# One more transfer per step and taller row-score matmuls in a one-core attention and FFN layer

## What is computed

```
xn = layernorm(x)
c_q, c_kv = xn @ Wq_down, xn @ Wkv_down          # latent 64
q_c, k_c, v_c = per head (128 heads) 4 features from the latents
q_r = xn @ Wq_rope  (128 heads x 64)             k_r = xn @ Wk_rope  (64, shared by all heads)
scores = (q_c . k_c + q_r . k_r) / sqrt(68)
out = softmax(scores) @ v_c, then @ Wo            -> s
g = silu(ffn(xn))                                 # low-rank adapted, tiled weights
y = x + s * g
```

## Time and profile before

| | us |
|---|---|
| median of 3 runs | 1936.92 |
| lowest, highest | 1936.13, 1938.21 |
| the profiled execution | 1934.79 |
| its span in the trace | 1932.6 |
| TensorE matmul busy | 1905.8 (99%) |
| VectorE busy | 1396.3 (72%) |
| ScalarE busy | 1028.6 (53%) |
| GpSimd busy | 467.9 (24%) |

### The profile page before, as it was taken

One profiled execution on the slowest core, in us unless ns is written; L12 is line 12 of the kernel. 1 busy time (PEld: TensorE's weight loads), 2 busy tenths in 40 slices (PEclk: granted clock), 3 DMA queues, 4 the chain that ended last, 5 costly groups with the idle time before them and its releaser, 6 DMA issues.

```text
span 1932.6 us, 37697 instructions
## 1 busy us (share of the span) xinstructions
PE 1905.8 (99%) x12464; PEld 1503.9 (78%) x12464; DVE 1396.3 (72%) x1644; ACT 1028.6 (53%) x1536; POOL 467.9 (24%) x790
## 2 busy tenths in 40 slices
PE   7999999999999999999999999999999999999999
PEld 5788777778777778777778877777877777777776
DVE  8787777777776777777777777777777777678665
ACT  5655555555555555555555555555555555555232
POOL 5422121222212131212122221213121212211231
PEclk9999999999999999999999999999999999999999
DMA  7622121221212121211121121212121212234331
GB/s 244 215 50 48 29 44 34 41 41 31 45 26 51 29 52 28 46 27 40 39 41 39 31 43 28 50 30 51 25 45 31 40 40 42 40 79 141 99 115 55
DMA packets 133963, 107.64 MB, mean 56 GB/s; under 512 B 52374, under 2 KB 97926, under 8 KB 133894
## 3 DMA queue, kind: packets, MB, share of 16 engines
q1 hardware_dynamic: 133870, 107.03, 23.5%
q10 hardware_dynamic: 48, 0.03, 0.0%
HBM read 52.80 MB, written 27.26 MB: 41 GB/s over the span
## 4 chain that ended last, share of the span: by engine, by line
PE 93%; SPq 2%; DVE 2%; DMA 1%; issue 1%; ACT 1%; POOL 0%; DVEq 0%; POOLq 0%; ACTq 0%
PE st L1009 24%; PE pj L1043 18%; PE ob L1043 18%; PE sx L1024 12%; PE ob L976 12%; PE ap L1681 2%; PE yp L1716 1%; PE zp L1716 1%; SPq L704 0%; PE zp L1666 0%; DMA slot<-mrow 0%; PE cp L575 0%; PE ob L993 0%; PE tp L567 0%; SPq L700 0%
## 5 line engine op out<-in xcount | busy, mean ns | idle before, releaser
L931 DVE TENSOR_REDUCE mx<-sx 128x4 fp32r<-128x1024 f32 x512 | 627.1, 1225 | 313.2 <-PE sx L1024 310.8
L912 ACT ACTIVATE probs<-st 128x1024 f32<-128x1024 f32 x512 | 492.3, 1011 | 149.5 <-PE ob L976 142.1
L794 POOL CAST k<-kc 64x512 fp32r<-64x512 f32 x256 | 155.9, 609 | 1067.8 <-PE st L1009 1067.5
L1009 PE MATMUL st<-slot,k 128*128 128x512 f32 x1024 | 408.4, 399 | 1.6 <-DMA slot<-mrow 1.6
L1009 PE MATMUL st<-slot,krlh 128*128 128x512 f32 x1024 | 400.8, 391 | 0.0
L1024 PEld LDWEIGHTS sx<-k,slot 88*128 88x128 f32 x2048 | 314.0, 190 | 51.7 <-issue 8.9
L1024 PE MATMUL sx<-k,slot 88*128 88x256 f32 x2048 | 329.6, 283 | 4.4 <-DMA slot<-kc 1.6
L866 ACT ACTIVATE slot<-pj 64x512 fp32r<-64x512 f32 x256 | 152.1, 594 | 314.5 <-PE pj L1043 311.4
L866 ACT ACTIVATE slot<-ob 64x512 fp32r<-64x512 f32 x256 | 152.0, 594 | 267.7 <-PE ob L1043 264.6
L976 PE MATMUL ob<-probs,vx 128*32 128x256 f32 x4096 | 234.9, 381 | 0.2 <-ACT probs L912 0.2
L1009 PEld LDWEIGHTS st<-slot,k 128*128 128x128 f32 x1024 | 192.3, 188 | 46.0 <-DMA slot<-mrow 3.0
(11 more groups left out here) (220 smaller groups left out, 1972.8 us busy)
## 6 DMA issues: line engine op xcount, KB each, us to landing
w_stage<-in_Wq_rope SPq DMA_DIRECT2D x64, 256.0 KB, 3.1
c_scratch<-stage SPq DMA_DIRECT2D x32, 256.0 KB, 3.1
c_in<-c_scratch SPq DMA_DIRECT2D x128, 64.0 KB, 2.0
o_scratch<-o_sb SPq DMA_DIRECT2D x128, 64.0 KB, 2.1
k<-kc SPq DMA_DIRECT2D x128, 48.0 KB
k<-kx SPq DMA_DIRECT2D x128, 48.0 KB
slot<-kx SPq DMA_DIRECT2D x256, 24.0 KB
slot<-kc SPq DMA_DIRECT2D x255, 24.0 KB
```

The source lines that it names most:

```text
L794: nc.gpsimd.tensor_copy(k1[0:64, s, :, :].rearrange("p a n -> p (a n)"), krh[:, bp * CH:(bp + 1) * CH]).then_inc(k_ready, 1)
L912: nc.scalar.activation(probs[:, k % NS, kt], st[:, kt], ACT.Exp, scale=SCALE).then_inc(exp_done, 1)
L931: nc.vector.tensor_reduce(mx[:, p, lo:lo + 4], sx[:, :, :].rearrange("p a (b k) -> p (a b) k", b=2), axis=AX.X, op=ALU.max).then_inc(red_d ...
L1009: last = nc.tensor.matmul(st[:, kt, h, :].rearrange("p (e n) -> p e n", e=PH), kk, q[:, s, :, h, :], start=(n == 0), stop=(n == 1))
```

## The change

For every step but the first four, `load_content` issues one more transfer, between the key content and the query content: row 89 of the slot (zero) is copied to row 88 of the same slot (4 KB, one partition to one partition). With row 88 zero, the row scores are taken over all 128 rows of `slot1` and `k1` instead of 88; the rows added contribute nothing. The two wait values on `ct_in` follow: three transfers in a slot's first turn, four in each later one.

```
+            if at.live(k - NS):
+                sp.dma_start(slot1[KC:KC + 1, s, :, :, :].bitcast(F32),
+                             slot1[KC + 1:KC + 2, s, :, :, :].bitcast(F32)).then_inc(ct_in[s], 16)
             for e in range(heads):
                 r = 64 + 12 * e
                 sp.dma_start(slot1[r:r + 12, s, e, :, :].bitcast(F32),
...
-                    pe.wait_ge(ct_in[s], 48 * (at.turn(k) + 1))
+                    pe.wait_ge(ct_in[s], 64 * at.turn(k) + 48)
...
-                                                slot1[0:KC, s, half, h, qt * 128:qt * 128 + 128], k1[0:KC, s, h, :],
+                                                slot1[:, s, half, h, qt * 128:qt * 128 + 128], k1[:, s, h, :],
...
-                sp.wait_ge(landed, 48 * NT)
+                sp.wait_ge(landed, 64 * (NT - 1) + 48)
```

## The result

The changed kernel takes 2009.8 us (median; 2009.1 to 2011.9) against 1936.5 us for the kernel before: a ratio of 1.0383, interval 1.0370 to 1.0396. It is 73 us slower. The sign, the mechanism and the steps in which it acts are those of the prediction; the size is 1.8 times the 41 us forecast, and the time lies just outside the range, which ended at 2007.

A forecast was written before the change was run, and what follows sets the result against it. The prediction took TensorE as the bound, with a chain of copy, SP issues and transfer close behind. Stalls of 45.4 us less 4 us for taller matmuls gave +41 us on 1936.9: 1978 us, range 1936 to 2007.

The forecast's parts named there:

- TensorE bound, with a second chain a few tenths behind: Whole kernel: TensorE sets the time; copy, SP issues and transfer run 0.20 to 0.49 us ahead of need in steps 1 to 3.
- Who waits: Row scores of a turn: step 1 stalls 0.27 us, step 3 0.39 us (0.59 in first turns), steps 2 and 0 nothing.
- The issue time: SP queue: issuing the one-row clearing takes 0.55 us, the middle of two other copies' 579 and 522 ns.
- The delay made of it: Row scores behind the clearing: their content comes later by the issue plus a 0.04 us gap, 0.59 us, before slack.
- The price of starting late: Row-score runs that start late: no term for a longer run, so nothing was added.
- The turns with staging: Step 3 in the 16 first turns of groups: no slack, so a turn pays 0.86 us instead of 0.66.
- The taller matmuls: Row scores over 128 rows instead of 88: 0.03 us gained per step, kept in two steps a turn, 4 us.
- The rival with delayed rings: Slot transfers also wait in the transfer engines behind the cleared row: 2016 us with 0.3 us more delay; chance 0.06.
- the rivals with a hidden clearing: Clearing costs TensorE nothing: with faster taller matmuls 1923 us, chance 0.11; with no difference from height 1937 us, chance 0.06.

The follow-up runs named there:

- the second transfer: Changed kernel plus a second transfer of the same shape behind the clearing, zero row 91 to zero row 90: 2099.4 us, ratio 1.0848.
- the pair of 68 and 4084 bytes: Changed kernel with only 17 elements (68 bytes) or 1021 elements (4084 bytes) cleared per step, each in one piece: 2016.1 us and 2015.3 us.
- the reordered kernel: Changed kernel with the clearing issued behind the two slot transfers and the attention-output store moved from s = 2 to s = 3: 1942.0 us, ratio 1.0042.

## Why the prediction was right in kind and wrong in size

*TensorE bound, with a second chain a few tenths behind.* Right. It needed only some 0.7 us more in that chain to put 19% of the critical chain on SP's queue.

*Who waits.* Right, by step: 1 and 3 stall, 2 is covered by the stall of 1, 0 by the value matmuls; the second transfer confirmed the rule at double the dose.

*The issue time.* The prediction took 0.55 us; it is 0.567 us. This term was right, though it was the middle of two other transfers' times and so lucky to come this close.

*The delay made of it.* This is the first step that failed. I set the delay of the row scores equal to the issue and its gap, 0.59 us. GpSimd's copies for steps 1 and 3, first before, then in the changed kernel:

```profile
939.59 0.61 POOL L794 CAST k<-kc 64x512 fp32r<-64x512 f32 x1 [7.61 <-PE st L1009]
950.83 0.61 POOL L794 CAST k<-kc 64x512 fp32r<-64x512 f32 x1 [2.52 <-PE st L1009]
```

```profile
977.85 0.61 POOL L797 CAST k<-kc 64x512 fp32r<-64x512 f32 x1 [7.58 <-PE st L1012]
989.56 0.61 POOL L797 CAST k<-kc 64x512 fp32r<-64x512 f32 x1 [3.44 <-PE st L1012]
```

Step 1: from the end of the copy to the end of the last slot issue it was 942.38 - 940.20 = 2.18 us before and is 981.37 - 978.46 = 2.91 us now, 0.73 us more; and from there to the matmul 2.12 us instead of the 2.09 I had from the earlier trace rows. That is 0.76 us in all, less the slack of 0.32: 0.44 us, against 5.97 - 5.54 = 0.43 measured. Step 3: it was 953.75 - 951.44 = 2.31 us and is 993.14 - 990.17 = 2.97 us, 0.66 us more; but from the last slot issue to the matmul it is only 2.06 us, 0.03 less than 2.09. That leaves 0.63 us less the slack of 0.20: 0.43 us, against 5.97 - 5.55 = 0.42 measured. Of the added 0.66 to 0.73 us, 0.61 are the issue and its gap; what is issued behind the clearing also got slower, the median of a slot issue by 34 ns (643 to 677). So the model was right and its delay too small: the two stalls of a turn without staging are 0.85 us instead of 0.66, and 64 x 0.19 = 12 us.

*The price of starting late.* The second missing term: each late run is 0.07 us longer (0.71 against 0.64). Twice a turn, 64 x 0.14 = 9 us. The prediction put it at nothing and gave no reason. The row that shows it stood in front of the prediction, the 0.71 us of the one late run of the earlier trace rows beside the 0.64 us of the earlier trace rows, and I read only its start.

*The turns with staging.* I gave 0.20 us more to the first turn of a group and left the rest "in the range". SP's queue behind the clearing delays step 3 in the first and in the last turn. The row scores of steps 2 and 3 in a first turn of the changed kernel:

```profile
961.67 0.64 PE L1027 MATMUL sx<-k,slot 128*128 128x256 f32 x4
...
967.98 0.71 PE L1027 MATMUL sx<-k,slot 128*128 128x256 f32 x4 [0.64 <-DMA slot<-kc]
```

It is 967.98 - 961.67 = 6.31 us between them, and not 5.97; in the last turn in front of it, 940.36 - 934.04 = 6.32 us. About 0.35 us in 32 turns are 11 us, where 16 x 0.20 = 3 us were forecast: 8 us. The experiment with the store moved shows the mechanism.

*The taller matmuls.* I gave them 4 us net of 8 gross. They are worth some 2 us in the kernel without the clearing, and next to nothing inside the changed kernel, where the time hangs on the other chain. That is 3 to 4 us of the miss. I had read a 9 ns difference of one product in the last stage as the property of the height; on the row scores it was 1 ns of 283.

By the Trainium skill, TensorE: Matmul & The Clock Gate, section "LDWEIGHTS (loading the stationary operand)", a load is paid by columns and not by rows. The runs agree within 1%, 190 ns over 88 rows and 188 ns over 128. Taken for the whole matmul, which the section doesn't claim, it would have been the better guide here than the row I preferred.

Sum: 41 + 12 + 9 + 8 + 4 = 74 us, against 2007.7 - 1932.6 = 75 us between the two spans. Most of the pieces are read from one or two turns, but means over all turns of fourteen groups give the same terms within about 1 us: 0.87 us a turn for the two stalls, 8.5 us for the late starts, 11 us for the turns with staging. The rival with delayed rings is refuted by the pair of 68 and 4084 bytes and by the distance from the last slot issue to the matmul, 2.06 to 2.12 us with the clearing and 2.09 without; the rivals with a hidden clearing by the timeline and by the time.

What stays open is why a slot issue takes 34 ns longer behind the clearing (654 to 662 ns behind the one of 17 elements), and what the last 7 us of the reordered kernel are.

## What to carry to other kernels

Here a transfer cost its place in the issuing queue and its bytes cost nothing. Write down, for each transfer that a busy engine waits for, the time from its trigger to its landing and how far ahead of need it lands, and put anything new behind those with the least slack and not in front of them. Follow the added time through the queue into the next step too, and give each late start its restart price. Before paying for a preparation (here clearing a row), ask whether the algebra needs it: a shift that is constant along the softmax didn't.

## What the runs showed of the hardware that I had not expected

- The time SP spends on an issue doesn't follow the bytes: 610 ns for 68 bytes as for 4084 bytes, each moved in one piece, and 567 ns for 4096 bytes, which the records show moved in 16 pieces of 256 bytes.
- The slot issues are longer behind a clearing, by their medians: 643 ns without one, 677 ns behind one, and 641 to 643 ns with the clearing behind them. It is not the only thing that lengthens them: with the clearing behind them, the first slot issue of the odd steps still took 0.69 us.
- With 4084 bytes cleared, the data of the row had moved 0.5 us before those of the slot transfers began to, on the median, though SP issued the two one right behind the other.
- A row-score run whose first weights come late takes 0.71 us instead of 0.64: one late start costs 0.07 us on top of the wait.
- Over 88 or 128 rows, a matmul of 256 columns differs by 1 ns of 283 and its load by 2 ns of 190.
